# Expert indices read into registers in groups, and the next weights' transfer placed ahead of a store, in a chain of four conditional layers

## The reference

```python
# layer 1, D = 128, E = 8, FF = 512, TOPK = 2, N = 2048 tokens
probs = softmax(h_flat @ router_w)
gates, idx = top_k(probs, TOPK)
gates = gates / gates.sum(-1, keepdims=True)
combine = zeros((N, E)).at[arange(N)[:, None], idx].add(gates)
hid = relu(einsum('nd,edf->nef', h_flat, exp_w1) + exp_b1)
eout = einsum('nef,efd->ned', hid, exp_w2) + exp_b2
y = einsum('ned,ne->nd', eout, combine)
x = x + y.reshape(x.shape)
# layer 2, one expert per sample, B = 64
h = gelu(einsum('bsh,bhi->bsi', x, Wi[expert_idx]) + bi[expert_idx][:, None, :])
r = einsum('bsi,bih->bsh', h, Wo[expert_idx]) + bo[expert_idx][:, None, :] + x
y = layernorm(r) * gamma[expert_idx][:, None, :] + beta[expert_idx][:, None, :]
```

## Time and profile before

| what | value |
|---|---|
| median of three runs | 327.73 us (327.21 to 332.39) |
| span of the profiled execution, from its first to its last instruction | 321.2 us |
| the profiled execution's own time | not given by the page beside the span |
| PE busy, share of the span | 247.4 us, 77% |
| DVE busy | 184.2 us, 57% |
| POOL busy | 129.6 us, 40% |
| ACT busy | 113.0 us, 35% |

### The profile page before, as it was taken

One profiled execution on the slowest core, in us unless ns is written; L12 is line 12 of the kernel. 1 busy time (PEld: TensorE's weight loads), 2 busy tenths in 40 slices (PEclk: granted clock), 3 DMA queues, 4 the chain that ended last, 5 costly groups with the idle time before them and its releaser, 6 DMA issues.

```text
span 321.2 us, 6590 instructions
## 1 busy us (share of the span) xinstructions
PE 247.4 (77%) x1630; PEld 195.3 (61%) x1630; DVE 184.2 (57%) x828; ACT 113.0 (35%) x393; POOL 129.6 (40%) x169
## 2 busy tenths in 40 slices
PE   4999999997548742888888859786843997998950
PEld 2656566445424632487778859786832886887840
DVE  1456656524989699244444525453522587897982
ACT  3343354225273313022222312221212664665640
POOL 6000000000152108465556535565347787778410
PEclk9999999955755655699999998999995999999985
DMA  5169600000050045237787775866745555656200
GB/s 140 27 168 317 177 2 0 1 2 0 0 132 0 2 131 161 30 75 210 199 204 192 205 200 144 184 200 189 201 106 152 152 150 152 171 132 161 75 24 19
DMA packets 38266, 38.42 MB, mean 120 GB/s; under 512 B 9491, under 2 KB 25909, under 8 KB 38230
## 3 DMA queue, kind: packets, MB, share of 16 engines
q1 hardware_dynamic: 32038, 26.18, 29.5%
q0 software_dynamic: 3360, 7.02, 10.8%
q10 hardware_dynamic: 2832, 4.80, 5.0%
HBM read 32.18 MB, written 6.19 MB: 119 GB/s over the span
## 4 chain that ended last, share of the span: by engine, by line
PE 53%; DVE 16%; DMA 10%; POOL 8%; issue 8%; ACT 2%; DVEq 0%; SPq 0%; ACTq 0%; POOLq 0%
PE bank L837 15%; PE bank L857 11%; PE bank L717 10%; DMA big<-expert_rows,xg 7%; PE bank L725 5%; POOL big L498 5%; PE bank L896 2%; PE bank L743 2%; DMA expert_rows<-es 2%; POOL ohp L451 2%; DVE x1r L1038 1%; DMA hg<-h_rows,map 1%; DVE bst L1043 1%; PE bank L893 1%; PE bank L833 1%
## 5 line engine op out<-in xcount | busy, mean ns | idle before, releaser
L837 PE MATMUL bank<-hgT,ws 128*128 128x128 f32 x488 | 68.5, 285 | 16.4 <-issue 9.9
L837 PEld LDWEIGHTS bank<-hgT,ws 128*128 128x128 f32 x488 | 61.2, 197 | 21.7 <-issue 13.4
L620 ACT ACTIVATE hid<-bank,bh 128x128 f32<-128x128 f32 x78 | 24.4, 364 | 84.4 <-PE bank L837 83.1
L481 POOL DMA_INDIRECT hg<-h_rows,map x39 | 37.0, 949 | 38.0 <-PE bank L833 30.9
L717 PE MATMUL bank<-ones 128*128 128x512 bf16 x176 | 49.2, 415 | 3.5 <-ACT trs L517 3.5
L498 POOL DMA_INDIRECT big<-expert_rows,xg x44 | 42.8, 973 | 15.0 <-issue 11.5
L857 PE MATMUL bank<-w,hid 128*128 x312 | 42.3, 279 | 0.3
L1174 DVE TENSOR_SCALAR hid<-bank,bh 128x128 f32<-128x128 f32 x78 | 23.8, 347 | 30.7 <-PE bank L837 30.6
L857 PEld LDWEIGHTS bank<-w,hid 128*128 128x128 f32 x312 | 38.6, 194 | 0.7 <-issue 0.7
L438 POOL TENSOR_SCALAR big<-x1r,rstd,nmr 128x128 f32<-128x128 f32 x8 | 3.5, 447 | 80.7 <-DVE nmr L1053 80.7
L717 PEld LDWEIGHTS bank<-ones 128*128 128x128 bf16 x176 | 18.9, 119 | 20.8 <-issue 5.9
(11 more groups left out here) (260 smaller groups left out, 363.8 us busy)
## 6 DMA issues: line engine op xcount, KB each, us to landing
ws<-in_L_cond_exp_w_dram SPq DMA_DIRECT2D x39, 256.0 KB, 3.4
ws<-in_L_cond_Wi_dram ACTq DMA_DIRECT2D x18, 256.0 KB, 3.1
b2blk<-in_L_cond_exp_b_dram SPq DMA_DIRECT2D x39, 64.0 KB, 3.8
expert_rows<-es SPq DMA_DIRECT2D x39, 64.0 KB, 3.8
out_dram<-yo SPq DMA_DIRECT2D x80, 16.0 KB
x_rows<-x1r SPq DMA_DIRECT2D x1, 1024.0 KB, 6.9
h_rows<-big SPq DMA_DIRECT2D x4, 256.0 KB, 2.4
ws<-in_L_cond_Wi_dram SPq DMA_DIRECT2D x4, 256.0 KB, 3.9
```

What stands on the lines that cost most here:

```text
L481: pool.indirect_dma_start(out=hg[:, b % RING, :], out_offset=None, in_=hdram, in_offset=bass.IndirectOffsetOnAxis(ap=map1[:, b:b + 1], axi ...
L620: last = act.activation(hid[:, u, c, :], ps[2 + u][:, c * P:(c + 1) * P], ACT.Relu, bias=bh1[:, c, b:b + 1])
L837: last = mm(ps[2 + 2 * (c // 2) + u][:, c % 2 * P:(c % 2 + 1) * P], ws[:, w, c * P:(c + 1) * P], hgT[:, u, :], start=True, stop=True)
```

## The change

A new helper, experts_in, reads several numbers of a table with one TENSOR_LOAD, followed by a register operation and a check for each number. With it:

- SP reads the numbers of blocks 0 to 3 in one group, those of blocks 4 to 23 in a group behind the transfer of x_rows, and those of blocks 24 to 38 in a group between block 19 and block 20.
- In SP's step of block b the transfer of the weights of block b+4 stands first, behind the wait for up_ps of block b, then the store of block b, then the bias row of block b+4.
- PE reads all 39 numbers in two groups, of 20 and 19, between the 12 filling products and the first transpose; the filling products wait for places as well.
- DVE reads its 22 numbers of layer 2 in one group ahead of the stage, ACT its 18 in one group ahead of the stage.

```diff
--- before.py
+++ after.py
@@ -263,7 +263,6 @@
         GS_SIDE = 3
         GS_RESP, GS_LONG = (26, 28, 29, 30), (GS_MASKS, GS_RANK2, GS_RANK2 + 1, GS_RANK2 + 2, GS_MAP2)
         SHARED = 4
-        FIRST2 = NB1 - NB2 - 2
         RESP_BANK = (1, 2, 5, 6)
         POOL_OH = 6
         N_SMALL, N_ROWS, N_CONST, N_SIDE = len(SMALL), len(ROWS), 17 + len(IOTAS), TILES + 6
@@ -303,6 +302,11 @@
             for j in range(n):
                 step(j, j % RING)
 
+        def experts_in(table, first, last, engine):
+
+            _, es_ = nc.values_load_multi_w_load_instructions(table[0:1, first:last], engines=[engine], min_val=0, max_val=E - 1)
+            return list(es_)
+
         def g128(t, g):
 
             return t[:, g * GT:(g + 1) * GT]
@@ -349,13 +353,8 @@
                 sp.dma_start(hdram[g * GW:(g + 1) * GW, :].rearrange("(i p) d -> p i d", p=P),
                              g128(hrow, g)).then_inc(h_stored, 16)
 
-            def weights1(b, r):
-                e = sp.value_load(bexi[0:1, b:b + 1], min_val=0, max_val=E - 1)
-                if b >= RING:
-                    sp.wait_ge(up_ps, b - RING + 1)
+            def weights1(b, r, e):
                 sp.dma_start(ws[:, r, :], exp_w1[bass.ds(e, 1), :, :].rearrange("e d f -> (e d) f")).then_inc(w1_ready[r], 16)
-                if b >= RING:
-                    sp.wait_ge(es_ready, b - RING + 1)
                 sp.dma_start(b2blk[:, r, :],
                              exp_b2[bass.ds(e, 1), :].rearrange("e d -> (e d)").partition_broadcast(P)).then_inc(b2_ready[r], 16)
 
@@ -364,16 +363,26 @@
                 sp.dma_start(edram[b * P:(b + 1) * P, :], es[:, r % 2, :]).then_inc(es_stored[r % 2], 16)
 
             def step1(b, r):
+                if b + RING < NB1:
+                    sp.wait_ge(up_ps, b + 1)
+                    sp.dma_start(ws[:, r, :], exp_w1[bass.ds(ahead[b], 1), :, :].rearrange("e d f -> (e d) f")).then_inc(w1_ready[r], 16)
                 store(b, r)
                 if b + RING < NB1:
-                    weights1(b + RING, r)
+                    sp.dma_start(b2blk[:, r, :],
+                                 exp_b2[bass.ds(ahead[b], 1), :].rearrange("e d -> (e d)").partition_broadcast(P)).then_inc(b2_ready[r], 16)
             sp.wait_ge(places, 1)
+            first = experts_in(bexi, 0, RING, mybir.EngineType.SP)
             for b in range(RING):
-                weights1(b, b)
+                weights1(b, b, first[b])
 
             sp.wait_ge(x_row_ready, 1)
             sp.dma_start(xdram[:, D:XW].rearrange("(i p) d -> p i d", p=P), x1r[:, :, D:XW]).then_inc(x_stored, 16)
-            blocks(NB1, step1)
+            ahead = experts_in(bexi, RING, RING + 20, mybir.EngineType.SP)
+            for b in range(20):
+                step1(b, b % RING)
+            ahead += experts_in(bexi, RING + 20, NB1, mybir.EngineType.SP)
+            for b in range(20, NB1):
+                step1(b, b % RING)
 
             def out_of_block(j, r):
                 samples_out(sp, mybir.EngineType.SP, j, r, range(SPT if j < NB2 - SHARED else SPT // 2))
@@ -620,8 +629,6 @@
                     last = act.activation(hid[:, u, c, :], ps[2 + u][:, c * P:(c + 1) * P], ACT.Relu,
                                           bias=bh1[:, c, b:b + 1])
                 last.then_inc(hidA_sb, 1)
-                if 0 <= b - FIRST2 < NB2 - RING:
-                    expert2.append(act.value_load(bex2i[0:1, RING + b - FIRST2:RING + b - FIRST2 + 1], min_val=0, max_val=E - 1))
 
             act.wait_ge(eqb_ready, 1)
             for i in range(TILES):
@@ -631,6 +638,7 @@
             act.wait_ge(bias_ps, 1)
             act.activation(bh1[:].rearrange("p c b -> p (c b)"), ps[6][:, 0:FC * NB1], ACT.Copy)
             act.activation(bh2[:].rearrange("p c b -> p (c b)"), ps[6][:, FC * NB1:FC * (NB1 + NB2)], ACT.Copy).then_inc(bias_ready, 1)
+            expert2 += experts_in(bex2i, RING, NB2, mybir.EngineType.Activation)
             act.wait_ge(bias_ready, 1)
             blocks(NB1, hidden)
 
@@ -848,7 +856,7 @@
 
             def down(b, r):
                 u = r % 2
-                e = pe.value_load(bexi[0:1, b:b + 1], min_val=0, max_val=E - 1)
+                e = expert1[b]
                 pe.wait_ge(hidA_sb, b + 1)
                 pe.wait_ge(hidB_sb, b + 1)
                 if b >= 2:
@@ -865,7 +873,10 @@
                 down(b, r)
 
             pe.wait_ge(ld_w2, 16)
+            pe.wait_ge(places, 1)
             busy(GATHER_BUSY)
+            expert1 = experts_in(bexi, 0, 20, mybir.EngineType.PE)
+            expert1 += experts_in(bexi, 20, NB1, mybir.EngineType.PE)
             rows_T(0, 0)
             rows_T(1, 1)
             up(0, 0)
@@ -1156,9 +1167,6 @@
                             ps[3][:, 2 * P:3 * P].rearrange("p (k i) -> p i k", i=TILES)).then_inc(x_row_ready, 1)
 
 
-            def expert(table, b):
-                return dve.value_load(table[0:1, b:b + 1], min_val=0, max_val=E - 1)
-
             def columns(b, r):
                 dve.wait_ge(row_T_ps, b + 1)
                 if b >= 2:
@@ -1187,17 +1195,14 @@
                 return t[:, bass.ds(e, 1), :].rearrange("p o d -> p (o d)")
 
 
-            expert2 = []
-
             def step1(b, r):
                 if b + 2 < NB1:
                     columns(b + 2, r + 2)
                 if b + 1 < NB1:
                     hidden(b + 1, r + 1)
                 rows_out(b, r)
-                if 0 <= b - FIRST2 < NB2:
-                    expert2.append(expert(bex2i, b - FIRST2))
-
+
+            expert2 = experts_in(bex2i, 0, NB2, mybir.EngineType.DVE)
             dve.wait_ge(bias_ready, 1)
             columns(0, 0)
             columns(1, 1)
```

## The result

| | before | changed |
|---|---|---|
| median on the same chip | 327.47 us (326.07 to 332.39, 4 runs) | 339.72 us (333.86 to 341.84, 4 runs) |
| ratio | 1 | 1.026, 95% interval 1.016 to 1.035 |
| span of the profiled execution | 321.2 us | 331.7 us |
| that execution's own time | not given | 333.86 us |

The changed kernel is slower by 2.6%; by the interval at least 1.6%. The profiled execution of the changed kernel was its fastest, at a mean granted clock of 0.851. Executions of 337.92, 341.51 and 341.84 us had 0.842, 0.833 and 0.828. They have no profile, so that the distance from the profile to the median is clock is inferred from this order and not shown.

The account below looks back on a forecast made before the run. PE's waits for late weights were taken to bound the expert stage. Costs of 6.6 + 2.4 + 3.0 less a gain of 13.1 gave -1.1 us: span 320.1, plus 6.5 makes 326.6 us, range 318 to 337.

Parts of the forecast that it names:

- (b): SP's grouped reads: the group of 15 in the middle of the stage delays a store, costing 3.0 us once.
- (d): Clock at the stage's start: after PE's idle time some 4.8 us at half speed lose 2.4 us.
- (a): Weights issued ahead in the expert stage: PE's wait for them goes, 2.56 to 2.22 us a block, gain 13.1 us.
- The store's loop: Two es buffers: es of block b+2 waits for block b's store; 4.15 us for two blocks, 2.08 a block.
- The first rival: Stores bind the stage harder as landings grow, deciding from 4.5 us a landing, 2.42 a block; 338 us, chance 0.16.
- The sign to look for: In the expert stage, DVE not waiting for the store with PE still idle would mean a wrongly named successor.
- (c): PE's 39 grouped reads before the first transpose take 11.7 us; the transpose moves from 137.1 to 143.7, 6.6 us lost.
- (e): DVE's and ACT's grouped reads ahead of the stage are hidden; DVE's would cost 1.8 us if PE's reads cost nothing.

Follow-up runs that it names:

- h1: The changed kernel itself, run again on a slower chip: 1.012 of the kernel before, stage 99.2 us.
- h3: The changed kernel with SP's group of 15 reads right behind its group of 20, ahead of block 0: 1.011 of the kernel before, stage 96.7 us.
- i2: The kernel before with weights ahead of the store, single reads and four buffers of es: 0.975 of the kernel before, stage 91.8 us.
- i3: The kernel before with weights ahead, single reads, two es buffers, stores issued by ACT, bias row one step later: 0.984 of before, stage 94.5 us.
- i4: The kernel before with weights ahead, single reads, four es buffers, stores issued by ACT, bias row one step later: 0.970 of before, 317.66 us.
- i1: The kernel before with weights ahead of the store alone, single reads, two buffers of es: 0.986 of the kernel before, stage 95.9 us.
- e1: The changed kernel with PE's reads put back singly in front of each w2 product: 1.010 of the kernel before, stage 105.1 us.

## Why the prediction was wrong

The forecast was 326.6 us in a range of 318 to 337; the median is 339.7. Of the four executions only the fastest, 333.86 us, lies within the range, and the forecast itself reached to 333.5. The predicted span was 320.1, the measured one 331.7. By the split above the 11.6 us are: 4.7 in the stage (a gain of 7.7 after (b) and (d) was forecast, 3.0 came), 1.6 at the reads (6.6 said, 8.2 came), 2.4 ahead of the change and 2.9 behind the stage, for both of which the sum had nothing. The last 1.5 us to the median are the distance from span to median, 8.0 us where 6.5 had been added.

(a) is the step that failed. It said of the weights: "They are now issued when L837 of block b is done, not after es of block b", and "this wait is gone, even with the longest landing". The wait of that transfer was read rightly, but not the queue in which it stands. In SP's order the weights of block b+4 stand behind the store of block b-1, and that store waits for es of block b-1. They were moved past one store, not past all: the distance from an es to its weights grew from three blocks to four, and no more. With the 3.4 us landing it had, that loop would have been (1.3 + 3.4 + 2.1) / 4 = 1.7 us a block, below the 2.22 that was forecast, so the missing link alone would not have bound. The second miss is that the forecast took the landings as they were: at the measured median of 4.75 us the loop is 2.0, and at the 5.9 us seen from block 10's weights to their product 2.3. The store's loop at its measured 4.2 us is 2.3. The stage without the stop of (b) took 94.2 / 39 = 2.42, an estimate that takes off the 2.5 us of h1 and h3. Neither loop gives that alone at its median landing; that two such loops hold a stage together is what i2, i3 and i4 show, there with single reads. The store's loop, which it named as the successor, was there (37 us of DVE's waiting in the changed kernel) and near what was forecast, 2.08; it wasn't alone. What (a) was worth is known from stages of different chips or executions only: 3.9 us (99.8 before, 95.9 in i1) or, from the changed kernel with (b)'s 2.5 taken off, 5.6 (99.8 to 94.2), in place of 13.1.

The first rival, stores that bind harder, had nearly the right time, 338 us, and half of the mechanism. That its time fits is partly luck, as 5.3 us of the loss, ahead of the change and behind the stage, stand in none of its terms. Its price was a landing of 4.5 us or more; the median store landed in 4.2. The pace came out at 96.7 / 39 = 2.48 with the stop of (b) in it, so past the 2.42 that the text gave as its mark; without the stop it is 2.42, just on it. The sign to look for, "if DVE does not wait for the store and PE is still idle", did not cover the case that came: DVE waits for the store and PE is still idle.

(b) said 3.0, with 4.2 us of reads. Measured: 5.4 us of reads, since the load of 15 takes 1.4 us and not 0.3, and 2.5 us of stage.

(c) said 143.7 for the first transpose, 12.0 us behind the filling products' start; it came 13.6 behind. Start and length were both off. The reads began at 133.0, 1.1 us before the first filling product, where the forecast had placed them 0.3 behind it. The Trainium skill ("TensorE: Matmul & The Clock Gate", "Architectural detail: the array is 16× 32×32, not 1× 128×128") gives TensorE's queue as 64 instructions. The trace agrees as far as it goes: the load started with both products L833 and twelve of L725 still to run, more than the six that the forecast had seen; no run shows where the queue is full. By that rule the start would have been 130.2, that is 1.5 us ahead, nearer than what was taken. The length was 14.6 us in place of 11.7: 39 pairs at 0.29, about as forecast, but 3.4 us for two loads in place of 0.8. The two errors partly cancel in the start of the stage.

(d) said 2.4 us. The clock was at half from 140.8 to 151.0, so 3.3 us of the stage, and the first ws product took 2.07 us in place of 1.06. At half speed 3.3 us of PE's work cost about 1.6, an estimate. But the kernel before had such a stretch in its stage too, at 190, and the changed one has none there: the mean granted clock of the whole stage is 0.98 in both, so over the stage (d) cost next to nothing. Not forecast: the filling products themselves ran at 0.62, 0.7 us, as they fell into the half-clock stretch that in the profile of before ended earlier.

(e) held. DVE's 22 reads ended at 143.6, hidden behind PE; e1 shows their price with that cover gone, 4.0 us, where 1.8 was said, mostly because of the load: 2.89 us in place of 0.3. ACT's lay in its idle time.

The chance of "slower" was 0.20, and the range ended 2.7 us short. The costs (b) and (c), 9.6 us by the forecast, were in the open and came as 10.7. The gain of 13.1 rested on a chain in which one link of SP's queue was missing and on landings that did not stay as they were.

## What to carry to other kernels

Where a transfer is moved ahead in a queue, write down everything that stands in front of it in that queue, over the border of the loop's step too: the store of the step before, with its wait, still holds it. And where two rings turn side by side, relaxing one shows little; before a limit is called innocent, relax both together (here 4.1 and 1.4 us alone, 14.7 together).

Reads of register values that ran beside PE's work cost nothing here: no idle time stood in front of the w2 products. Grouped ahead of a stage, they were a serial stretch of about 0.37 us a number in front of everything. On the engine that starts the stage that is the worst place.

## What the hardware showed that had not been expected

- A load of several numbers into registers takes longer than one of a single number: 0.30 us for one, 0.51 for 4 and 1.41 for 15 (SP), 1.56 for 20 and 1.86 for 19 (PE), 1.67 for 18 (ACT), 2.06 for 20 (SP), 2.89 for 22 (DVE). The count is not all, as PE's two show. That is 0.07 to 0.12 us for each number beyond the first. The Trainium skill ("Runtime: NRT & Kernel Launch", "Instruction fetch mechanics") says that such loads cost about 200 ns for each register, there of registers loaded from the chip's large memory; here, from a table in the memory on the core, it is a third to two thirds of that, but the cost for each register is there.
- PE's queue began to read registers 1.1 us ahead of the first of twelve filling products, and with two products more still to start (the changed kernel, 133.0).
- The same kernels differ by chip: 327 us on two occasions and 353 to 356 on three, nearly all of it behind the expert stage.
- A stage that became 10.6 us shorter gave 6.6 us back behind itself (i4 beside i2, on one chip), with a longer wait for POOL's gathers of the next layer's rows and a clock at half for longer.
